# A masked graph-attention layer: four weight buffers on VectorE in visits 1 to 7, and the making of h drawn together into visits 1 to 17

## What is computed

```python
def _L0_gnn_ref(h, adj, a):
    d = h.shape[1]
    h1 = h @ a[:d]
    h2 = h @ a[d:]
    e = jax.nn.leaky_relu(h1 + h2.T, negative_slope=0.01)
    attention = jnp.where(adj > 0, e, NEG_BIG)
    attention = jax.nn.softmax(attention, axis=1)
    return attention @ h

h = jnp.maximum(_layernorm(x, axis=-1), 0.0)
x = x + _L0_gnn_ref(h, adj, L0_gnn_a)
```

## Time and profile before

| what | value |
|---|---|
| time, median of 3 runs | 1552.17 us (1550.98 to 1555.96) |
| the profiled execution | 1552.08 us, of which the span is 1550.3 us |
| granted TensorE clock, mean | 0.999 |
| TensorE matmuls busy | 1522.7 us (98%) |
| VectorE busy | 1489.6 us (96%) |
| ScalarE busy | 1162.5 us (75%) |
| GpSimd busy | 457.4 us (30%) |

### The profile page before, as it was taken

One profiled execution on the slowest core, in us unless ns is written; L12 is line 12 of the kernel. 1 busy time (PEld: TensorE's weight loads), 2 busy tenths in 40 slices (PEclk: granted clock), 3 DMA queues, 4 the chain that ended last, 5 costly groups with the idle time before them and its releaser, 6 DMA issues.

```text
span 1550.3 us, 38852 instructions
## 1 busy us (share of the span) xinstructions
PE 1522.7 (98%) x12678; PEld 1511.9 (98%) x12678; DVE 1489.6 (96%) x2172; ACT 1162.5 (75%) x1180; POOL 457.4 (30%) x547
## 2 busy tenths in 40 slices
PE   5999999999999999999999999999999999999999
PEld 5999999999999999999999999999999999999998
DVE  7999999999999999999999999999999999999998
ACT  7787877778777777677776876777777777677774
POOL 6363334335452340120420320320320320420420
PEclk9999999999999999999999999999999999999999
DMA  6666677787778799999999999999999999999994
GB/s 211 222 200 230 206 223 227 230 248 221 245 220 254 220 225 233 221 201 206 218 207 207 224 204 207 226 197 210 230 195 205 228 195 207 217 195 209 219 199 98
DMA packets 436493, 331.05 MB, mean 214 GB/s; under 512 B 16704, under 2 KB 378176, under 8 KB 436416
## 3 DMA queue, kind: packets, MB, share of 16 engines
q1 hardware_dynamic: 411360, 288.94, 83.6%
q10 hardware_dynamic: 25056, 41.13, 8.7%
HBM read 308.90 MB, written 21.10 MB: 213 GB/s over the span
## 4 chain that ended last, share of the span: by engine, by line
PE 82%; DMA 5%; DVE 3%; ACT 3%; issue 2%; SPq 1%; ACTq 0%; DVEq 0%
PE acc L950 27%; PE acc L953 26%; PE acc L952 26%; DMA adj_in<-in_adj_dram 5%; PE T L917 2%; ACT mask L542 2%; DVE w_lo L797 1%; DVE halves L786 1%; SPq L268 1%; ACT w_hi L552 0%; DVE T L767 0%; DVE w_lo L801 0%; ACT w_hi L555 0%; DVE adj_in L901 0%; DVE adj_in L896 0%
## 5 line engine op out<-in xcount | busy, mean ns | idle before, releaser
L950 PE MATMUL acc<-h_hi,w_hi 128*128 128x258 f32 (+1 forms) x4096 | 1167.3, 285 | 9.2 <-DVE w_lo L801 3.4
L953 PE MATMUL acc<-h_hi,w_lo 128*128 128x258 f32 (+1 forms) x4096 | 1153.3, 282 | 0.0
L952 PE MATMUL acc<-h_lo,w_hi 128*128 128x256 f32 (+1 forms) x4096 | 1149.7, 281 | 0.0
L950 PEld LDWEIGHTS acc<-h_hi,w_hi 128*128 128x128 f32 x4096 | 771.8, 188 | 17.8 <-issue 8.0
L952 PEld LDWEIGHTS acc<-h_lo,w_hi 128*128 128x128 f32 x4096 | 778.4, 190 | 0.1
L953 PEld LDWEIGHTS acc<-h_hi,w_lo 128*128 128x128 f32 x4096 | 775.3, 189 | 0.0
L786 DVE SCALAR_TENSOR_TENSOR halves<-r_rep,g_all,T 128x512 f32<-128x512 f32 (+1 forms) x1024 | 712.7, 736 | 10.8 <-PE T L917 1.5
L542 ACT ACTIVATE mask<-adj_in,mhalf 128x2048 fp8e5<-128x2048 int32 x256 | 510.3, 1993 | 58.8 <-DMA adj_in<-in_adj_dram 58.5
L552 ACT ACTIVATE w_hi<-halves 128x1024 fp32r<-128x1024 f32 x336 | 353.6, 1057 | 185.0 <-DVE halves L786 172.3
L797 DVE SCALAR_TENSOR_TENSOR w_lo<-halves,w_hi 128x1024 fp32r<-128x1024 f32 x336 | 418.2, 1245 | 9.9 <-PE acc L953 4.9
L555 ACT ACTIVATE w_hi<-halves 128x1024 fp32r<-128x1024 f32 x176 | 185.3, 1057 | 97.5 <-DVE halves L786 92.6
(11 more groups left out here) (70 smaller groups left out, 343.8 us busy)
## 6 DMA issues: line engine op xcount, KB each, us to landing
adj_in<-in_adj_dram SPq DMA_DIRECT2D x672, 256.0 KB, 5.0
adj_in<-in_adj_dram SPq DMA_DIRECT2D x88, 1024.0 KB, 6.3
part_sums<-stage ACTq DMA_DIRECT2D x24, 516.0 KB, 5.6
xo<-part_sums ACTq DMA_DIRECT2D x24, 516.0 KB, 4.4
r_rep<-r_rows SPq DMA_DIRECT2D x39, 256.0 KB, 4.8
xb<-in_x_dram ACTq DMA_DIRECT2D x15, 512.0 KB, 5.9
out_dram<-xb ACTq DMA_DIRECT2D x15, 512.0 KB, 4.7
xb<-in_x_dram SPq DMA_DIRECT2D x14, 512.0 KB, 5.8
```

The source lines that it names most:

```text
L950: nc.tensor.matmul(acc[:, t, 0:WC], w_hi[:, k % HL, cols], rhs_hi, start=start and u == 0, stop=False)
L952: nc.tensor.matmul(acc[:, t, 0:D], w_hi[:, k % HL, cols], rhs_lo, start=False, stop=False)
L953: last = nc.tensor.matmul(acc[:, t, 0:WC], w_lo[:, k % LL, cols], rhs_hi, start=False, stop=stop and u == 1)
```

## The change

- `DEEP` is 18 instead of 22: the turned load, VectorE's transposes and the four deep buffers begin with visit 18, and `N_MID` follows.
- Chunks 4 to 11 of h are made one a visit in visits 1 to 8; chunks 12 to 15 one in each two visits, 9 and 10 to 15 and 16. Visit 17 finishes chunk 15. Before, chunks 8 to 15 took visits 5 to 20, and visit 21 finished.
- In visits 1 to 7 (`wide`) there are four weight buffers: `xo` is laid behind `halves` in one tensor `work`, and its first 1024 words serve as parts 8 and 9. The upper half of each pair has a place of its own (parts 3, 5, 8, 9); the lower half uses parts 2 and 4 by turns. `weights` writes the upper half first, waiting only for the subtraction of pair g - 4, then the lower half, waiting for that of pair g - 2.
- In these visits `scores` can't use `xo` as scratch: its first product goes to the unused half of the PSUM tile `hs_ps`, its second to part 2 or 4, for which it waits for the subtraction of pair g - 2.
- In a visit with `phase="whole"`, `round_h` rounds all four tiles in step 2, none in step 0.

```diff
-    N_MID = 2 * 22
+    DEEP = 2 * SH + 2
+    N_MID = 2 * DEEP
...
-        halves = sb("halves", [P, 8, BLK], f32)
+        work = sb("work", [P, 8 * BLK + G * WC], f32)
+        halves = work[:, 0:10 * BLK].rearrange("p (n j) -> p n j", j=BLK)
         W = halves[:, 2:6, :].rearrange("p (k u) j -> p k (u j)", u=2)
+        xo = work[:, 8 * BLK:].rearrange("p (t w) -> p t w", w=WC)
+        wide_w = [halves[:, 2:4, :], halves[:, 4:6, :], halves[:, 2:9:6, :], halves[:, 4:10:5, :]]
...
-            quarter(0, 0, None, head=True, dt=0, dt_next=0)
-            quarter(1, 0, "first", make=Q, phase="whole", dt=0, dt_next=0)
-            with eng.Fori(2, 5) as v:
-                quarter(v, 0, "first", make=v + 3, phase="whole", made=v + 2, dt=0, dt_next=0)
-            two(0, 0, 0, "first", "first", dt=0)
-            two(1, 0, 1, "first", "first", nxt=0)
-            with eng.Fori(2, 5) as j:
-                two(j, 1, 1, "added", "added")
-            two(5, 1, 2, "added", "added", nxt=0)
-            with eng.Fori(6, 8) as j:
-                two(j, 2, 2, "added", "added")
-            quarter(21, 2, "added", made=NB - 1, dt_next=LATE)
+            def two(v, c, q1, q2, nxt=None, dt_next=MID):
+                quarter(v, q1, "added", make=c, phase="early", made=c - 1, nxt=nxt)
+                quarter(v + 1, q2, "added", make=c, phase="late", turn=q2 != q1, dt_next=dt_next)
+
+            quarter(0, 0, None, head=True)
+            quarter(1, 0, "first", make=Q, phase="whole", wide=True)
+            with eng.Fori(2, SH - 1) as v:
+                quarter(v, 0, "first", make=v + 3, phase="whole", made=v + 2, wide=True, pwide=True)
+            quarter(SH - 1, 0, "first", make=SH + 2, phase="whole", made=SH + 1, nxt=0, wide=True, pwide=True)
+            quarter(SH, 1, "first", make=SH + 3, phase="whole", made=SH + 2, turn=True, pwide=True)
+            with eng.Fori(0, 3) as j:
+                two(SH + 1 + 2 * j, SH + 4 + j, 1, 1)
+            two(2 * SH - 1, NB - 1, 1, 2, nxt=0)
+            quarter(DEEP - 1, 2, "added", made=NB - 1, dt_next=LATE)
...
-            quarter(22, 2, "added", dt=LATE, dt_next=LATE, deep=True)
-            quarter(23, 2, "added", nxt=0, dt=LATE, dt_next=LATE, deep=True)
+            quarter(DEEP, 2, "added", dt=LATE, dt_next=LATE, deep=True)
+            with eng.Fori(DEEP + 1, NPART - 1) as v:
+                quarter(v, 2, "added", dt=LATE, dt_next=LATE, deep=True)
+            quarter(NPART - 1, 2, "added", nxt=0, dt=LATE, dt_next=LATE, deep=True)
...
-                    if k == 0:
+                    if k == 0 and V.phase != "whole":
                         round_h(V.made, 0, [0, 1])
                     if k == 2:
-                        round_h(V.made, 0, [2, 3])
+                        round_h(V.made, 0, range(G) if V.phase == "whole" else [2, 3])
...
+                        if free is not None and j == 1:
+                            dve.wait_ge(s_lo, free)
...
-                if wait and (not V.deep or enter):
+                if wait and not V.wide and (not V.deep or enter):
                     dve.wait_ge(s_lo, g - 1)
...
-                for u in range(2):
+                for u in (1, 0) if V.wide else (0, 1):
                     e = 2 * (k % 2) + u
+                    if V.wide and u == 1:
+                        dve.wait_ge(s_lo, g - 1 if enter else g - 3)
+                    if V.wide and u == 0:
+                        dve.wait_ge(s_lo, g - 1)
+                        if scored is not None:
+                            dve.wait_ge(s_dot, scored)
...
+                def row_sums(e):
+                    if V.wide:
+                        if isinstance(V.v, int) and V.v == 1 and e == 0:
+                            dve.wait_ge(s_hsum, Q)
+                        scores(V.make, 0, [e], [hs_ps[:, D:2 * D], wide_w[e][:, 0, 0:D]], g - 1)
+                    else:
+                        scores(V.make, 0, [e])
```

## The result

The changed kernel took 1558.17 us in the median of 6 runs (1555.03 to 1569.36), the kernel before 1552.34 in the same sessions: a ratio of 1.0046 (95% interval 1.0026 to 1.0066). A second set of 12 runs gave 1.0027 (1.0013 to 1.0040). So the change costs 4 to 7 us. The forecast was +1.0, 1553.1 us, with a range up to 1557.0; the median lies 1.2 us outside it. The profiled execution of after is the fastest of its six: 1555.03 us, span 1552.9, that is 2.95 us above the profiled one of before.

What follows compares the result with a forecast made beforehand. TensorE bounds `two` and good deep visits, VectorE's waits add 1.18 us to whole ones, DMAs limit visits 22 to 24. 103.02 (whole) + 94.8 (deep) - 196.8 (removed) = +1.0, from 1552.1 to 1553.1 us; range 1544.5 to 1557.0.

Steps and rivals of the forecast that it cites:

- X: Time of a whole visit with wide buffers after the change: 25.79 us, against 25.78 before.
- the 0.18 at the loop border: VectorE's extra loss between two loop rounds; visits 7 and 8, outside a loop, were to save 0.18 us each.
- the ring: Whole visit's chain through ScalarE's rounding of h, normalised tile and VectorE's row sums; forecast 0.10 us later than before.
- the wait in step 4: VectorE's first row sum waiting for ScalarE's first normalised tile in whole visits; forecast to remain, about 0.9 us in all.
- Rival 1: Whole visits come down to TensorE's pace, 24.60 us, if ScalarE's chain has slack; 1545.0 us in all; chance 0.22.
- Rival 5: GpSimd holds step 5's subtraction fully in each whole visit: +3.3 us, 1556.4 us in all; chance 0.08.
- Rival 3: Wide form removes nothing, the 0.19 us in whole visits being there without the wait: +1.1, 1554.2 us; chance 0.08.
- the rule that the prediction set against the change: On VectorE a semaphore between two operations costs nothing extra; the wide form would save nothing, the sum 1.1 us higher.
- the lead: Deep visits: DMAs' lead used up in visits 18 and 19, then four visits pay 23.70 us each, 94.8 us.
- Rival 2: DMAs keep pace in deep visits, 22.79 us each: -3.6 against the sum, 1549.5 us; chance 0.10.
- rival 4: Every deep visit behind the lead takes 25.39 us, four costing 101.6 instead of 94.8; 1559.9 us; chance 0.12.
- Visits 9 to 17 are as 9 to 17 were: Visits 9 to 17 keep 24.60 us each, the last with two groups of transposes less; no term in the sum.

Runs made afterwards that it cites:

- e3: Changed kernel with h rounded two tiles in step 0 and two in step 2, as before the change: 1553.35 us, ratio 1.0013 to the kernel before.
- e4: Changed kernel without the wide buffers in any visit: 1559.61 us, ratio 1.0049 to the kernel before.
- e14: Changed kernel loading and adding only one of four row tiles of part sums, other sums left out: 1544.29 us, ratio 0.9951 to the kernel before.
- e15: Changed kernel with the whole load of part sums, but GpSimd adding only one of four row tiles: 1557.48 us, ratio 1.0045 to the kernel before.
- e1: Changed kernel run again with no edit: 1557.11 us, ratio 1.0027 to the kernel before.
- e9: Kernel before with 32 unused bytes a partition ahead of w_hi, moving w_hi, w_lo and all behind: 1554.33 us, ratio 1.0019 to the kernel before.
- e10: Changed kernel with w_hi and w_lo allocated ahead of the joined tensor: 1558.02 us, ratio 1.0032 to the kernel before.
- e16: Repeat of e10, changed kernel with w_hi and w_lo allocated first: 1557.91 us, ratio 1.0047 to the kernel before.
- e11: Changed kernel, w_hi and w_lo first, h rounded two and two, first normalised tile ahead of the pair's rounding: 1549.72 us, ratio 0.9981 to the kernel before.
- e8: Kernel before with the first normalised tile ahead of the pair's rounding in whole visits: 1548.92 us, ratio 0.9990 to the kernel before.

## Why the prediction was wrong

**Whole visits: right.** X was to be 25.79; it is 25.71. Visits 5 to 8 take 102.80 us, where 103.02 was worked out, and nothing came of visits 2 to 4 either, as said. The mechanism is in the main the one named: what the wide buffers save is taken by the wait for the normalised tile, which ScalarE's new order makes later (e3 and e4 undo one each: -4.6 and +0.85 us in visits 2 to 8). Details were off and cancelled: the 0.18 at the loop border belonged to the wait and went with it (visits 7 and 8 are only some 0.04 us shorter than the looped ones), and the ring goes through TensorE and the evacuation as well, so that the wait in step 4 is 1.46 us and not 0.9. Rival 1 needed slack in ScalarE's chain; there is none. Rival 5 didn't come: the rest of h starts at 113.77 us in visit 3 and its last tile ends before step 5's subtraction starts (117.07), which lasts 1.22. Timeline of GpSimd after:

```profile
113.77 2.83 POOL L404 TENSOR_TENSOR h_lo<-work,h_hi 128x256 f32 x4 [1.46 <-ACT h_hi L521]
```

Rival 3 is refuted by the 1.15 and 1.13, and with it the rule that the prediction set against the change, for this case. The Trainium skill, VectorE: DVE Perf Modes, section "The DRAIN you can't avoid", has from a run of eight copies that a semaphore between them costs nothing extra; the same section adds that a next operation that is not held starts earlier. The second is what the trace agrees with here: 1.15 us from start to start in step 3 without the wait, 1.32 with it, in the earlier trace rows as in e4.

**Deep visits: the limit right, its price 0.9 us too low.** The prediction let two of six visits run on the lead (23.23 and 23.07 us) and the other four take 23.70 each, 94.8 in all; with visit 24 as it was, that makes 166.5 us for visits 18 to 24. They took 167.37 and 167.42: 46.9 instead of 46.3 in visits 18 and 19, and 95.0 and 95.2 in 20 to 23. Visits 22 to 24 alone, which had the turned load before, too, rose from 71.69 to 72.60 and 72.05. That the DMAs' traffic is the limit was argued then and is shown now, by e14 and e15. Rival 2 (22.79 each) is what e14 has to leave out part of the load to get (22.90 at its placement), and rival 4 (25.39 each) didn't come.

**The step that failed is a term put at nothing.** "Visits 9 to 17 are as 9 to 17 were", says the prediction, and the final visits aren't in its sum at all. Visits 25 to 38 took 1.1 us more than before in the first profile of after and 3.2 more in e1, the one close to the median. One thing that the sum left out is shown: joining `halves` and `xo` moves `w_lo` by 32 bytes within 128, and every undisturbed visit at TensorE's pace is longer, 24.63 instead of 24.60, 22.90 instead of 22.79, 91.60 instead of 91.35 for 32 pairs. Over the visits 9 to 17, the seven final visits of 8 pairs from 26 on and the eight of 32 pairs that is 0.3 + 0.8 + 2.0 = 3.1 us; the same move alone costs the kernel before 2.5 us (e9). The diff shows this line, and the prediction read it only for what the buffers hold.

The final visits feel the DMA limit as well: e14 gains 6.6 us in visits 18 to 24 and 4.8 us in visits 25 to 38 over its control. But they did so before the change, too, and no run shows that the change made it worse there: from 652 to 1450 us the conversions waited for adj 31.9 us before, 25.9 after and 44.3 in e1.

With +1.9 to +2.1 measured in visits 2 to 24 and 2.8 for the placement in the final visits, some 5 us are accounted for, where two sets of runs measured 4.2 and 7.1 by their ratios. That isn't a clean division: undoing the placement in the changed kernel (e10, e16) gave the pace back but no time; visits 18 to 24 and the short final visits got longer instead. It is not that a faster TensorE waits longer for adj in the final visits: the conversions waited 27.4 and 24.0 us there, no more than in after. Why these visits lose, and so what the placement is worth in the changed kernel, stays open; the final visits of single executions of one kernel differ by 4 us (805.3 and 809.6 in these two), too much for a profile to settle it.

**Chances.** Slower by more than 0.3%, as the first set of runs has it (the second has 0.27%), had 0.15, from rivals 4 and 5. Neither is the cause. No rival was about TensorE's pace, since nothing in the change seemed to touch TensorE.

## What to carry over

Ask what an edit sets free and who is next in that chain: four buffers removed a wait that was exposed twice a visit, and the engine whose order was changed in the same edit took the time back; where two edits meet in one ring, undoing them one at a time prices each. A tensor that is resized moves all that is allocated behind it, so compare the pace of stretches whose code is unchanged before reading anything into the total. And when the transfers are behind, look at the traffic before the order of the engines: here 9.5 MB less, of 331, gave 13 us (in a kernel that leaves sums out, so this is a bound and no version to use), and the best order tried gave 8 (e10 to e11).

## What the runs showed of the hardware

TensorE's pace hangs on the place of `w_lo`, a weight operand, in SBUF: 118.7 ns a matmul at the old place, 119.3 with 32 bytes more, and 22.97 instead of 22.79 us for 8 pairs with 64 more; moving `w_lo` without `w_hi` is enough for 22.88, and moving both by -16384 bytes leaves 22.79.

A subtraction on VectorE with both inputs in SBUF takes 1.22 us alone and up to 1.8 beside GpSimd's reads. Which of the two loses depends on a fraction of a microsecond: in step 2 of visits 3 to 6 of the changed kernel a sum on GpSimd (L395) starts some 0.66 us ahead of the subtraction, which takes 1.22, and the next sum takes 1.65; in e4 the sum starts 0.31 ahead, and the subtraction takes 1.51.

A wait's row can be less than what the wait costs. In e8 the row of 0.20 us went away and a visit got 0.29 shorter: from subtraction to row sum it is 1.54 from start to start instead of 1.81, since an instruction that waits for nothing starts 0.08 before the record of the subtraction ahead of it ends.
